# Sums turned by 128-column transposes, scores issued behind the turned tiles, ScalarE masks at the end of a slot

## The reference

```python
qkv = (xn @ Wqkv.T + bqkv)                 # q, k layer-normalised over the 8 channels of a head
aw = softmax(q @ k.T / sqrt(8))            # 256 x 256 for each head
kth = top_k(aw, 12)[..., -1:]              # the 12th largest of each row
aws = aw * (aw >= kth); aws /= aws.sum(-1) + 1e-8
o_s = aws @ v
o_l = (softmax(q) @ (softmax(k).T @ v)) / (z + 1e-6)
o = a * o_s + (1 - a) * o_l                # a = sigmoid(alpha), one for each head
y = x + o @ Wproj.T + bproj + (xn @ W[idx] + b[idx])
```

## Time and profile before

| what | value |
|---|---|
| median of 3 runs | 1219.39 us |
| the profiled execution: time | 1222.3 us |
| its span, first to last instruction | 1220.5 us |
| mean granted TensorE clock | 0.962 |
| busy: VectorE / ScalarE / TensorE / GpSimd | 94% / 87% / 83% / 82% |
| instructions | 34803 |

### The profile page before, as it was taken

The page is one execution under the profiler, slowest core; times in us unless marked ns, Lnnn a source line. Parts: engine busy times, 40 slices in busy tenths (PEclk is TensorE's granted clock), DMA queues, the critical chain, the costliest instruction groups (busy, mean ns, idle before and its releaser), DMA issues.

```text
span 1220.5 us, 34803 instructions
## 1 busy us (share of the span) xinstructions
PE 1011.5 (83%) x9381; PEld 707.2 (58%) x9412; DVE 1151.5 (94%) x4358; ACT 1065.0 (87%) x3474; POOL 995.2 (82%) x1972
## 2 busy tenths in 40 slices
PE   4578888888888888888888888888888888888888
PEld 1356556656556556556655656656556655656655
DVE  6999999999999999999999999999999999999994
ACT  3689898999989899998899989899989898989884
POOL 5688888888888888888888888888888888888863
PEclk9989999999999899999999999899999999999988
DMA  3122222122222122222122222122222122222110
GB/s 101 42 65 66 84 83 79 37 67 70 84 83 83 37 62 70 84 84 84 36 68 65 84 84 83 37 62 71 83 84 82 38 72 61 84 79 79 44 46 10
DMA packets 165126, 82.79 MB, mean 68 GB/s; under 512 B 7737, under 2 KB 164927, under 8 KB 164930
## 3 DMA queue, kind: packets, MB, share of 16 engines
q1 hardware_dynamic: 164658, 80.43, 22.8%
q10 hardware_dynamic: 272, 0.13, 0.0%
HBM read 42.78 MB, written 37.75 MB: 66 GB/s over the span
## 4 chain that ended last, share of the span: by engine, by line
POOL 32%; PE 27%; ACT 19%; issue 15%; DVE 5%; DMA 1%; DVEq 0%; POOLq 0%; ACTq 0%; SPq 0%
ACT e L879 12%; POOL gap L437 10%; POOL below L441 5%; PE turn_ps L1051 5%; PE pv_ps L1073 3%; POOL qkn L359 3%; PE work_ps L1156 3%; POOL qk_b L359 3%; PE pv_ps L1084 3%; DVE top L654 3%; PE turn_ps L1052 2%; POOL drop L412 2%; PE work_ps L1144 2%; PE work_ps L1187 2%; POOL sq_half L422 2%
## 5 line engine op out<-in xcount | busy, mean ns | idle before, releaser
L879 ACT ACTIVATE e<-score_ps,drop 128x256 f32<-128x256 f32 x1024 | 475.2, 495 | 31.1 <-POOL drop L412 30.9
L1051 PE MATMUL turn_ps<-ident,e 128*128 128x128 f32 x2016 | 401.9, 293 | 21.0 <-ACT part L863 17.5
L661 DVE MATCH_REPLACE8 rest<-e 128x256 f32<-128x256 f32 x1020 | 415.9, 412 | 0.0
L667 DVE MAX8 next<-rest 128x8 f32<-128x256 f32 x1020 | 410.4, 419 | 0.5 <-issue 0.3
L654 DVE MAX8 top<-score_ps 128x8 f32<-128x256 f32 x1024 | 362.0, 419 | 34.4 <-PE score_ps L1033 34.1
L1052 PE MATMUL turn_ps<-minus_huge,below 128*128 128x128 bf16 x2016 | 380.0, 226 | 0.0
L437 POOL TENSOR_SCALAR gap<-e,next 128x256 bf16<-128x256 f32 x794 | 368.9, 479 | 0.0
L1051 PEld LDWEIGHTS turn_ps<-ident,e 128*128 128x128 f32 x2016 | 296.8, 147 | 59.3 <-issue 21.7
L839 ACT ACTIVATE kept<-turn_ps 128x1024 f32<-128x1024 f32 x252 | 267.5, 1062 | 56.9 <-PE turn_ps L1052 56.9
L441 POOL TENSOR_SCALAR below<-gap 128x768 bf16<-128x768 bf16 (+1 forms) x254 | 216.7, 853 | 41.4 <-POOL gap L437 41.4
L879 ACT ACTIVATION_READ_ACCUMULATOR e<-score_ps,drop 128x1 f32 x1024 | 232.9, 227 | 0.0
(11 more groups left out here) (229 smaller groups left out, 1439.6 us busy)
## 6 DMA issues: line engine op xcount, KB each, us to landing
part_slots<-part SPq DMA_DIRECT2D x128, 192.0 KB, 2.3
q_slots<-part_slots SPq DMA_DIRECT2D x64, 256.0 KB, 3.5
k_slots<-part_slots SPq DMA_DIRECT2D x64, 256.0 KB, 4.2
part_slots<-part SPq DMA_DIRECT2D x64, 128.0 KB, 1.9
x_sb<-in_L_attn_x SPq DMA_DIRECT2D x32, 128.0 KB, 4.0
x_res<-in_L_attn_x SPq DMA_DIRECT2D x32, 128.0 KB, 4.2
out_y<-out_sb SPq DMA_DIRECT2D x32, 128.0 KB, 4.4
w_ops<-in_L_ffn_W SPq DMA_DIRECT2D x1, 512.0 KB
```

The lines of the kernel that those rows point to most:

```text
L661: nc.vector.match_replace(rest[:, t, :], e8[:, (u_ - 1) % 2, t, :], e[:, (u_ - 1) % RING, t, :], REMOVED).then_inc(s["rest_ready"], 1)
L667: nc.vector.max(next8[:, (u_ - 1) % RING, t, :], rest[:, t, :]).then_inc(s["next_ready"], 1)
L879: nc.scalar.activation(e[:, u_ % RING, t, :], score_ps[:, u_ % 2, t // 2, t % 2, :], ACT.Exp, bias=drop[:, u_ % 2, t, 0:1], accum_out=z[:, ...
L1051: mm(dst, e[:, r, t, keys], ident[:], start=True, stop=False, is_transpose=True)
```

## The change

1. **Sums.** `gather` grows from 36 to 128 columns, so that it is a permutation of all 128 rows. The eight matmuls against it become transposes of 128 columns each, which overlap in PSUM and add up (the surplus columns carry zeros). The two matmuls for the denominators become one with 32 columns. The same is done in the epilogue.
2. **TensorE's order in a slot.** Before: turn, product, (sums in slot 5), early, scores, late. After: turn; product in slots 0 and 4; early in slots 3, 5 and 6; scores; product in slots 2 and 6; early in slots 0 and 7; sums in slot 5; late; early in slot 1. Early of slot 4 does nothing before or after.
3. **ScalarE's order in a slot.** The mask tile (L892) moves from right behind `e8` to the end of the slot, behind all copies of the slot. The copy `osT` (L851, slot 1) moves from ahead of the exponentials to behind them.

```diff
-        gather = sb("gather", [P, 4 * VA])
+        gather = sb("gather", [P, P])
...
-            used = gather[:].rearrange("p (j e) -> p j e", e=VA)
+            used = gather[:, 0:4 * VA].rearrange("p (j e) -> p j e", e=VA)
+            spare = gather[:, 4 * VA:].rearrange("p (j e) -> p j e", e=VW - VA)
             select(used, ALU.not_equal, 1.0, 0, [[-VW, 4], [-1, VA]], 1, 7).then_inc(s["gather_ready"], 1)
+            select(spare, ALU.not_equal, 1.0, -VA, [[-VW, 4], [-1, VW - VA]], 1, 7).then_inc(s["gather_ready"], 1)
...
-                    if u_ == 1 and exists(it - 2):
-                        act.wait_ge(s["w_osT"], it - 1)
-                        nc.scalar.copy(osT[:], pv_ps[:, 0:N]).then_inc(s["osT_copied"], 1)
...
-                    if exists(it if u_ >= 2 else it - 1):
-
-                        r = (u_ - 2) % RING
-                        act.wait_ge(s["next_ready"], TILES * (g - 1))
-                        for t in range(POOL_TILES[r], TILES):
-
-                            nc.scalar.activation(below[:, r, t, :], e[:, r, t, :], ACT.Relu, scale=-1.0,
-                                                 bias=next8[:, r, t, TOPK - 9:TOPK - 8]).then_inc(s["below_act"], 1)
...
                         nc.scalar.copy(sums_sb.rearrange("p g e -> p (g e)"), pv_ps[:, 0:NT * H * VA]).then_inc(
                             s["sums_copied"], 1)
+                    if u_ == 1 and exists(it - 2):
+                        act.wait_ge(s["w_osT"], it - 1)
+                        nc.scalar.copy(osT[:], pv_ps[:, 0:N]).then_inc(s["osT_copied"], 1)
...
                         nc.scalar.copy(qk_raw[:], work_ps[:]).then_inc(s["raw_ready"], 1)
+                    if exists(it if u_ >= 2 else it - 1):
+
+                        r = (u_ - 2) % RING
+                        act.wait_ge(s["next_ready"], TILES * (g - 1))
+                        for t in range(POOL_TILES[r], TILES):
+
+                            nc.scalar.activation(below[:, r, t, :], e[:, r, t, :], ACT.Relu, scale=-1.0,
+                                                 bias=next8[:, r, t, TOPK - 9:TOPK - 8]).then_inc(s["below_act"], 1)
...
-                            mm(pv_ps[:, at:at + 4 * VA], oT[:, nxt, q // 2, 1 - q % 2, t * P:(t + 1) * P], gather[:],
-                               start=(t == 0 and q == 0), stop=False, skip_group_check=True)
+                            mm(pv_ps[:, at:at + P], oT[:, nxt, q // 2, 1 - q % 2, t * P:(t + 1) * P], gather[:],
+                               start=(t == 0 and q == 0), stop=False, is_transpose=True, skip_group_check=True)
...
-                    for t in range(NT):
-                        over_t = pv_ps[:, t * H * VA:(t + 1) * H * VA].rearrange("p (h e) -> p h e", e=VA)[:, :, D]
-                        last = mm(over_t, eps_ident[:], z[:, nxt, t, :], start=False, stop=True, skip_group_check=True)
-                    last.then_inc(s["w_turn"], 1)
+                    mm(pv_ps[:, 0:NT * H * VA].rearrange("p (g e) -> p g e", e=VA)[:, :, D], eps_ident[:],
+                       z[:, nxt].rearrange("p t h -> p (t h)"), start=False, stop=True,
+                       skip_group_check=True).then_inc(s["w_turn"], 1)
...
-                    if u_ % 2 == 0 and exists(it if u_ >= 6 else it - 1):
+                    if u_ in (0, 4) and exists(it - 1):
                         product(u_)
+                    if u_ in (3, 5, 6) or u_ == 7 and it < 0:
+                        early(u_)
+                    if exists(it if u_ < UNITS - 1 else it + 1):
+                        scores(u_)
+                    if u_ in (2, 6) and exists(it if u_ >= 6 else it - 1):
+                        product(u_)
+                    if u_ == 0 or u_ == 7 and it >= 0:
+                        early(u_)
                     if u_ == 5 and exists(it - 1):
                         sums()
-                    early(u_)
-                    if exists(it if u_ < UNITS - 1 else it + 1):
-                        scores(u_)
                     late(u_)
+                    if u_ == 1:
+                        early(u_)
```

More of the change, by code:

```diff
@@ L1152, in early @@
                             pe.wait_ge(s["pool_const"], 7)
-                            pe.wait_ge(s["gather_ready"], 3)
+                            pe.wait_ge(s["gather_ready"], 4)
                         for t in range(NT):
@@ L1321, in _ @@
             sums_ps = turn_ps[:, 0].rearrange("p m n -> p (m n)")
-            for t in range(NT):
-                over_t = sums_ps[:, t * H * VA:(t + 1) * H * VA].rearrange("p (h e) -> p h e", e=VA)[:, :, D]
-                mm(over_t, eps_ident[:], z[:, side, t, :], start=(t == 0), stop=False, skip_group_check=True)
+            mm(sums_ps[:, 0:NT * H * VA].rearrange("p (g e) -> p g e", e=VA)[:, :, D], eps_ident[:],
+               z[:, side].rearrange("p t h -> p (t h)"), start=True, stop=False, skip_group_check=True)
             for q in range(QUADS):
@@ L1328, in _ @@
                     at = (t * QUADS + q) * 4 * VA
-                    last = mm(sums_ps[:, at:at + 4 * VA], oT[:, side, q // 2, 1 - q % 2, t * P:(t + 1) * P], gather[:],
-                              start=False, stop=(q == QUADS - 1), skip_group_check=True)
+                    last = mm(sums_ps[:, at:at + P], oT[:, side, q // 2, 1 - q % 2, t * P:(t + 1) * P], gather[:],
+                              start=False, stop=(q == QUADS - 1), is_transpose=True, skip_group_check=True)
             last.then_inc(s["w_turn"], 1)
```

## The result

The changed kernel takes 1256.69 us (median of 4 runs, 1253.37 to 1259.71); the kernel before, run beside it, 1221.86 (4 runs, 1219.28 to 1228.09). The ratio is 1.028, 95% interval 1.023 to 1.033: 2.8% slower. The forecast was 1204 with a range up to 1231. What came is the rival called *Slower*, at 1245, and 12 us past it.

What follows compares the result with a forecast made beforehand. VectorE, 94% busy, was taken as the bound: 35.08 + 0.2 + 0.25 + 0.65 = 36.18 us an iteration against 36.52. That gives 10 us by 30 iterations, 15 with the end: 1207 profiled, 1204 median, range 1184 to 1231.

Steps and rivals of the forecast that it cites:

- Slower: Rival: scores of slot 0 hold q and k until a late load, clock low, ScalarE passes it on; about 1245 us; chance 0.14.
- The floor: VectorE's own work in an iteration, 35.08 us; 1.44 us on the mean lie above it in the kernel before.
- Sums: Slot 5: eight transposes take 1.0 us and the single denominator matmul 0.3; some 1.0 us of TensorE saved.
- Scores ahead at slots 6 and 7: Scores of slot 7 come 1.3 to 2.5 us earlier; VectorE's waits there go, 1.58 us in slow iterations, 0.37 in fast.
- Masks at the end: ScalarE's slots: moving the 0.39 us mask saves nothing in all, but what stood behind it comes earlier by that.
- Scores of slot 0 ahead of q and k: Slot 7: load lands 0.3 us before due, a late one costs 0.9; taken as 0.25 an iteration, 45% late.
- TensorE's clock: Idle time in slot 7 lowers the clock at slot 0 in half the iterations, at 1.3 us: 0.65 an iteration.
- `e8`: ScalarE, in arrears because q and k come later, delivers `e8` of slot 1 late: 0.2 us, bounds 0 and 0.4.
- The end: End of the run: 4 us back from one 5.5 us wait for scores, 1 in the epilogue's sums; bounds 2 and 6.
- Transposes don't keep the clock up: Rival: the clock falls in each iteration, at the turn of slot 0 too; 1225 us; chance 0.08.
- `top` waiting at slot 0 in under half of the iterations: Sign named for the forecast: VectorE's `top` waits at slot 0 in fewer than half of the iterations.

Runs made afterwards that it cites:

- no_load: Changed kernel, but scores of slot 0 made from the batch already loaded, without waiting for the load (two heads of each batch wrong): 1168.15 us, ratio 0.954.
- sums_only: Kernel before with only the new sums (128-column transposes, one denominator product), both orders as before: 1196.39 us, ratio 0.980.
- fill8: Changed kernel with eight unread 128x512 matmuls ahead of TensorE's wait for the load in slot 7: 1223.39 us, ratio 0.997.
- qk_first: Changed kernel with one part undone: in slot 7 TensorE makes q and k ahead of the scores of slot 0 again: 1193.32 us, ratio 0.976.
- after_first2: Changed kernel with the first load cut from four slots to two (`FIRST` 4 to 2): 1204.44 us, ratio 0.987.

## Why the prediction was wrong

**The step that failed** is what the scores of slot 0 cost when they stand ahead of q and k: the load's lateness and TensorE's clock, put at 0.25 + 0.65 = 0.90 us an iteration and added up as if one had nothing to do with the other. They came to 0.62 + 1.64 = 2.26. The mechanism was named rightly, a late load and a fall of the clock behind the idle time; how often and how much, and how the second hangs on the first, was not.

**The floor was right.** 35.08 us of VectorE's own work an iteration: `no_load` runs at 35.06.

**Sums.** Put at 1.3 us for eight transposes and the denominator product; they take 1.24 from 593.02 to 594.26 in `sums_only`. What I left out is what they do to the clock: with them alone it no longer fell at slots 5 and 6, 24 us with what they save at the end. In the prediction this gain was booked to the scores going ahead. The run with the old sums shows that it isn't: 13.5 us come back.

**Scores ahead at slots 6 and 7.** The waits of 0.99 and 0.37 us at slot 7 went, as said. But `sums_only`, with the old order, has 0.4 us of `top` waits left at slot 7 in the whole run: the new sums do it without the order, and the order alone, with the old sums, hides half of the falls.

**Masks at the end.** Put at nothing; worth 14 us beside the new sums.

**Scores of slot 0 ahead of q and k.** The sum took the load to land 0.3 us before it was due, by one iteration in which the write had landed early, and a late one at 0.9 in 45% of iterations. `top` waited in 17 of 29, 1.05 us on the mean and up to 2.2: 0.62 an iteration where the sum had 0.25. The iteration of the earlier trace rows is one of the 19 with an early write: from the end of the part's cast to the issue of `k_slots` 3.0 us pass there, so about 2.6 to that of `q_slots`, which goes 0.4 ahead; in the other 10 it is 3.4 to 4.1, and in the changed kernel up to 4.7. A margin of 0.3 doesn't hold against that.

**TensorE's clock.** Taken as a fall in half of the iterations at 1.3 us each, 0.65. This is the term with the largest error. It fell in 24 of 29 at the turn of slot 0, and the waits for the scores of slot 1 that follow are 2.0 us on the mean and reach 3.29, 1.64 an iteration. I had the slowed turn in (1.2 us) and, as a bound, part of q and k (1.9). Missing was product 0, which stands behind the turn and ahead of the scores of slot 1, 0.84 us more (1.91 against 1.07), and above all that late load, slowed q and k, turn and product are one chain: they add in the same iteration. `fill8` and `qk_first` show it: with the clock up, or with q and k ahead of the load, `top` hardly waits at slot 1 however late the load is.

**`e8`.** Put at 0.2, bounds 0 and 0.4: `rest` waits 0.4. The arrears of ScalarE that were to come from q and k did not reach VectorE; in the kernel before `rest` waited 0.5 an iteration.

**The end.** Put at 5 us, bounds 2 and 6; it gave 8.9 (57.46 against 48.55).

**The sum once more.** Against the prediction, the late load costs 11 us more in 30 iterations, the clock 30, `e8` 6, VectorE's own instructions 4 (35.23 against 35.08), and the end gives 4 more: 47 of the 48 us between 1207 and the profiled 1255.35.

**The rivals.** *Slower* had the right place and the right point of decision, 1.44 us of additions; they came to 2.81 against its 2.4. Its last step was wrong: ScalarE passing the delay on through `e8`. The delay went from TensorE straight to `top`, by the scores of slot 1. That it came within 12 us is partly luck: it put the late load at 0.9 an iteration (0.62) and the clock at 1.3 (1.64), errors that go against each other. *Transposes don't keep the clock up* did not come about: in the changed kernel the clock stays up behind all 31 sums. Of the signs named, `top` waiting at slot 0 in under half of the iterations failed: it was 17 of 29. What went wrong is the weighing: each of the two terms was taken in the middle between its bounds, as if they were independent and as if one iteration gave the margin. 0.3 us of margin under a transfer whose start scatters over 2 us is no margin, and the queue behind it held everything that the clock could slow down.

## What to carry to other kernels

In a queue that is worked in order, work that needs nothing from a load belongs ahead of the wait for it: q and k, 1.7 us of matmuls, on the wrong side cost 63 us in 30 iterations here, with the clock that fell behind the wait. Where a step rests on a landing time, take from the trace the spread of that time over all iterations before setting a margin, and add up what stands behind the wait in the queue, at the low clock. And test the parts of a change alone: this one held two gains, of 24 and 14 us, and a loss that hid both; the cheapest cure, a smaller first load, was not in it at all.

## What was not expected of the hardware

- A write that is read back through memory has a wide spread: SyncE waited 1.5 us for the landing of the parts in one iteration and 3.6 in another, and from the end of the cast to the scores 6.2 to 8.7 us pass. The times fall in two groups: from the cast to the issue of `q_slots` 2.6 us in 15 of 29 iterations, 3.4 to 4.7 in 14. What decides between them no run shows.
- Halving the first load from 256 to 128 KB a side shortened the landing of `k_slots` from a median of 3.2 us to 2.3 (the change against `after_first2`); with 64 KB it was 2.0.
- After idle times of 1.8 to 4.4 us the granted clock fell in 24 of 29 iterations, but not by length alone: a wait of 1.83 us was followed by no fall, one of 1.90 by one, one of 2.71 by none.
- A fall costs by what stands behind it. 10 falls at slot 0 in `qk_first` made `top` wait 0.35 us at slot 1, 24 in the changed kernel 47.6.
- Sums of 36-column matmuls with the denominators, 2.4 us behind 1.07 us idle, were followed by a fall in 18 of 31 cases; transposes of 128 columns, 1.24 us with the denominators behind the same 1.07, in none. That it is the columns and not the shorter time was not told apart.
